# First attention of a two-layer language-model tower: the values of two of eight key tiles in fp16 parts made by GpSimd, with a factor in the row of maxima

## The reference, cut to what matters

```python
scores = jnp.einsum('bshc,bthc->bsth', q, k) * SCALE
A = jax.nn.softmax(scores, axis=2)
u = jnp.einsum('bsth,bthc->bshc', A, val).reshape(B, S, H * C)
return u @ Wout + bout
```

## Time and profile before

| what | value |
|---|---|
| median of three runs | 4917.46 us |
| the profiled execution's own time | 4918.01 us |
| its span | 4916.3 us |
| the first attention, from its first instruction to its last | some 677 to 2853 us |
| PE busy over the span | 4586.0 us, 93% |
| DVE, ACT, POOL busy | 3655.1, 3150.1, 2325.2 us |

### The profile page before, as it was taken

How to read it: one execution, slowest core, us unless ns; L and a number is a source line. 1 busy time by engine, 2 the same in 40 slices (tenths; PEclk the granted TensorE clock), 3 DMA queues, 4 the chain that set the end, 5 groups by cost and what they waited for, 6 DMA issues and landing times. The chain is left out here.

```text
span 4916.3 us, 106442 instructions
## 1 busy us (share of the span) xinstructions
PE 4586.0 (93%) x42579; PEld 2033.3 (41%) x42579; DVE 3655.1 (74%) x6356; ACT 3150.1 (64%) x3450; POOL 2325.2 (47%) x2279
## 2 busy tenths in 40 slices
PE   5999969999999999999999979999999999999965
PEld 3433423333333333333333334444444444444433
DVE  4677756666666666666666678888888888888878
ACT  2444426666666666666666638888888888888844
POOL 3455553333333323233333346666666666666656
PEclk9999979999999999999999979999999999999966
DMA  4212100000000000000000000000000000000001
GB/s 102 69 52 69 35 1 1 1 1 1 1 1 1 1 1 1 1 1 1 1 1 1 1 1 2 2 2 2 2 2 2 2 2 2 2 3 2 2 7 28
DMA packets 43624, 51.44 MB, mean 10 GB/s; under 512 B 33416, under 2 KB 33544, under 8 KB 43144
## 3 DMA queue, kind: packets, MB, share of 16 engines
q1 hardware_dynamic: 40440, 44.03, 3.4%
q10 hardware_dynamic: 2704, 0.72, 0.1%
HBM read 39.73 MB, written 4.19 MB: 9 GB/s over the span
## 5 line engine op out<-in xcount | busy, mean ns | idle before, releaser
L1716 DVE TENSOR_REDUCE a_mp<-psum 128x1 f32<-128x512 f32 x2072 | 1324.8, 685 | 667.8 <-PE psum L1593 654.1
L2442 DVE TENSOR_REDUCE f_mp<-psum 128x1 f32<-128x512 f32 (+2 forms) x2352 | 1472.7, 684 | 187.1 <-PE psum L2264 171.0
L1561 ACT ACTIVATE a_prob<-psum,escale 128x1024 f32<-128x1024 f32 x1024 | 1086.3, 1110 | 524.6 <-PE psum L1642 524.6
L2224 ACT ACTIVATE f_prob<-psum,escale_f 128x1024 f32<-128x1024 f32 x1152 | 1247.2, 1112 | 217.1 <-PE psum L2341 108.4
L1650 PE MATMUL psum<-a_prob,a_v 128*64 128x512 f32 x4104 | 994.2, 605 | 0.0
L2078 POOL TENSOR_SCALAR f_hi<-f_raw,part 128x512 f16<-128x512 f32 x324 | 506.2, 1562 | 393.8 <-ACT f_raw L2182 387.5
L2264 PE MATMUL psum<-f_kf,f_qf 64*128 64x512 f16 (+2 forms) x3658 | 652.6, 307 | 40.1 <-DVE f_mp L2442 31.2
L1481 POOL TENSOR_TENSOR a_u<-a_og,a_inv 128x512 f32<-128x512 f32 x129 | 134.4, 1042 | 1167.4 <-DVE a_inv L1731 1167.4
L2354 PE MATMUL psum<-f_prob,f_vh 128*32 128x512 f32 (+3 forms) x6144 | 614.7, 495 | 9.3 <-DVE f_oc L2464 7.3
L2333 PE MATMUL psum<-f_qf,f_kf 64*128 64x512 f16 (+3 forms) x3074 | 505.5, 327 | 18.9 <-ACT f_og L2187 18.2
L1650 PEld LDWEIGHTS psum<-a_prob,a_v 128*64 128x64 f32 x4104 | 249.0, 136 | 505.1 <-issue 501.5
(11 more groups left out here) (448 smaller groups left out, 6942.4 us busy)
## 6 DMA issues: line engine op xcount, KB each, us to landing
idx<-in_itok_BS_dram SPq DMA_DIRECT2D x36, 512.0 KB, 6.0
idx<-in_itok_BS_dram SPq DMA_DIRECT2D x54, 256.0 KB, 6.9
idx<-in_x_dram SPq DMA_DIRECT2D x18, 256.0 KB, 3.6
a_qh<-a_rowT SPq DMA_DIRECT2D x258, 1.0 KB
out_dram<-h SPq DMA_DIRECT2D x16, 256.0 KB, 2.6
f_qf<-f_rowT SPq DMA_DIRECT2D x130, 4.0 KB, 1.7
wd<-in_L_ffn_Wd_dram SPq DMA_DIRECT2D x2, 256.0 KB
bd<-in_L_ffn_bd_dram ACTq DMA_DIRECT2D x16, 2.0 KB
```

The source lines that it names most:

```text
L1561: act.activation(prob[:, part], k.psum[:, pair:pair + 2].rearrange("p b n -> p (b n)"), ACT.Exp, scale=k.escale[:]).then_inc(s.read, 1)
L1716: dve.tensor_reduce(mp[:, tg % 2, t + 4 * r, c:c + 1], bank_of(j + r), X, ALU.max)\
L2224: act.activation(prob[:, u % NPF], k.psum[:, pair:pair + 2], ACT.Exp, scale=k.escale_f[:])\
L2442: dve.tensor_reduce(side[:, at[0]:at[-1] + 1:step], bank_of(j + r)[:, 0:len(at) * width].rearrange("p (a b) -> p a b", b=width), X, ALU.ma ...
```

## The change

Key tiles 2 and 4 no longer go through fp32. GpSimd makes `ph`, an fp16 copy of their `a_prob`, and `pl`, the fp16 rest (`halve`, 128x1024 each); once per batch it makes the same of `a_v` (`twice`, into `vh`, `vl`). PE forms their values in three pairs of fp16 matmuls (vl by ph, vh by pl, vh by ph). The chunks become `(0, 1), (3,), (2, 5), (4, 6, 7)`, at the same places. A constant `level`, 6 ln 2 divided by the scale of Exp and at most 8192, is added to the row of maxima when it is copied (a `tensor_scalar` in place of the copy), so that the weights come out 64 times larger. On GpSimd `add` now comes one round later than before, directly behind the halving of key tile 2; `prepare_batch` and `split_x` stand behind it, and the halving of key tile 4 behind these. Three semaphores of an earlier phase are used again, and four buffers are cleared at the start.

```diff
-A_PARTS = ((0, 1), (2, 3), (4, 5), (6, 7))
+A_PARTS = ((0, 1), (3,), (2, 5), (4, 6, 7))
+A_PART_OF = {kt: p for p, part in enumerate(A_PARTS) for kt in part}
+A_HALVED = {2: 0, 4: 1}
+A_LEVEL = 6 * math.log(2.0)
+A_LEVEL_MOST = 8192.0
...
+                def twice(b, par, n):
+
+                    here = v[:, par, :, 0]
+                    pool.tensor_copy(vh[:, par], here).then_inc(s.p, 1)
+                    passed(pool, k.seen, s.p, n + 5)
+                    pool.tensor_tensor(vl[:, par], here, vh[:, par], ALU.subtract).then_inc(s.p, 1)
+
+                def halve(G, kt, count):
+
+                    at = A_HALVED[kt]
+                    passed(pool, k.seen, s.read, count)
+                    pool.tensor_copy(ph[:, at], prob[:, kt]).then_inc(s.p_high, 1)
+                    passed(pool, k.seen, s.p_high, n_half(G, kt))
+                    pool.tensor_tensor(pl[:, at], prob[:, kt], ph[:, at], ALU.subtract).then_inc(s.p_low, 1)
...
                 pool.memset(v[:, 1], 0.0).then_inc(s.clear, 1)
-                pool.sem_inc(s.summed, 1)
-                pool.sem_inc(s.scaled, 2)
-                pool.wait_ge(s.clear, 6)
+                pool.memset(ph[:], 0.0).then_inc(s.clear, 1)
+                pool.memset(pl[:], 0.0).then_inc(s.clear, 1)
+                pool.memset(vh[:, 1], 0.0).then_inc(s.clear, 1)
+                pool.memset(vl[:, 1], 0.0).then_inc(s.clear, 1)
...
                 prepare_batch(0, 0, 0)
+                twice(0, 0, 0)
...
                     for x in range(AROUND):
                         G = i * AROUND + x
+                        b = i * 2 + x // HEADS + 1
+                        split_q(G + 2, (x + 2) % 4, n_stream(i, x, "q", 0))
+                        halve(G, 2, n_stream(i, x, "exp", 2))
+                        if G > 1:
+                            add(i * 2 + (x - 2) // HEADS, x % 2, G)
+                        if x % HEADS == 4:
+                            prepare_batch(b, (x // HEADS + 1) % 2, b * 6)
+                        if x % HEADS == 5:
+                            split_x(b, (x // HEADS + 1) % 2, n_stream(i, x, "x", 0))
+                        halve(G, 4, n_stream(i, x, "exp", 4))
                         if x % HEADS == 3:
                             squares(i * 2 + x // HEADS)
-                        if x % HEADS == 4:
-                            b = i * 2 + x // HEADS + 1
-                            prepare_batch(b, (x // HEADS + 1) % 2, b * 4)
-                        for n, kind, of, part in STREAMS[x]:
-                            if kind == "out":
-                                add(i * 2 + (x - 1) // HEADS, (x + 1) % 2, G + 1)
-                            elif kind == "x":
-                                split_x(i * 2 + x // HEADS + 1, (x // HEADS + 1) % 2, n_stream(i, x, kind, part))
-                            elif kind == "q":
-                                split_q(G + of, (x + of) % 4, n_stream(i, x, kind, part))
+                        if x % HEADS == 6:
+                            twice(b, (x // HEADS + 1) % 2, b * 6)
...
                     for kt in A_PARTS[p]:
+                        if kt in A_HALVED:
+                            at = A_HALVED[kt]
+                            pe.wait_ge(s.p_low, n_half(G, kt))
+                            for a, b in ((vl, ph), (vh, pl), (vh, ph)):
+                                for half in range(2):
+                                    last = pe.matmul(ps[A_SUM][halves(half)], lhsT=a[:, bp, kt],
+                                                     rhs=b[:, at, half * HALF:(half + 1) * HALF],
+                                                     start=False, stop=False, skip_group_check=True)
+                            continue
...
-                        dve.tensor_copy(rowT[:, tg % 2], bank_of(j)[0:T].bitcast(FP16)[:, 0:P]).then_inc(s.row_out, 1)
+                        dve.tensor_scalar(rowT[:, tg % 2], bank_of(j)[0:T].bitcast(FP16)[:, 0:P], level[0:T], None, ALU.add)\
+                           .then_inc(s.row_out, 1)
```

More of the change, by code:

```diff
@@ L1 @@
 from contextlib import ExitStack
+import math
 import numpy as np
@@ L704, in layer0 @@
         E = {name: k.sem("l0_" + name) for name in L_EVENTS}
+        k.spent, k.spent_at = [E[name] for name in ("gT", "eg", "wT")], PAIRS_
         def first(pair):
@@ L1345, in attention1 @@
         prob = sb("a1_prob", [P, NPB, S], F32)
+        ph = sb("a1_ph", [P, 2, S], FP16)
+        pl = sb("a1_pl", [P, 2, S], FP16)
+        vh = sb("a1_vh", [P, 2, T, C], FP16)
+        vl = sb("a1_vl", [P, 2, T, C], FP16)
+        level = sb("a1_level", [P, 1], F32)
         un = sb("a1_un", [P, HALF], F32)
@@ L1366, in attention1 @@
         s.q_split = k.sem("a1_q_split")
+        s.p_high, s.p_low, s.level = k.spent
         s.inverse = k.sem("a1_inverse")
@@ L1394, in n_pv, with n_half @@
             return NAV * (G + 1) + p + 1
+        def n_half(G, kt):
+            return k.spent_at + 2 * (G + 1) + A_HALVED[kt] + 1
         def bank_of(j):
@@ L1499, in _ @@
                 pool.memset(v[:, 1], 0.0).then_inc(s.clear, 1)
-                pool.sem_inc(s.summed, 1)
-                pool.sem_inc(s.scaled, 2)
-                pool.wait_ge(s.clear, 6)
+                pool.memset(ph[:], 0.0).then_inc(s.clear, 1)
+                pool.memset(pl[:], 0.0).then_inc(s.clear, 1)
+                pool.memset(vh[:, 1], 0.0).then_inc(s.clear, 1)
+                pool.memset(vl[:, 1], 0.0).then_inc(s.clear, 1)
+                pool.sem_inc(s.summed, 2)
+                pool.sem_inc(s.scaled, 3)
+                pool.sem_inc(s.p_high, 2)
+                pool.sem_inc(s.p_low, 2)
+                pool.wait_ge(s.clear, 10)
                 prepare_batch(0, 0, 0)
+                twice(0, 0, 0)
                 split_x(0, 0, 1)
@@ L1509, in _ @@
                         G = i * AROUND + x
+                        b = i * 2 + x // HEADS + 1
[8 more added lines that the diff above has]
+                        halve(G, 4, n_stream(i, x, "exp", 4))
                         if x % HEADS == 3:
                             squares(i * 2 + x // HEADS)
-                        if x % HEADS == 4:
-                            b = i * 2 + x // HEADS + 1
-                            prepare_batch(b, (x // HEADS + 1) % 2, b * 4)
-                        for n, kind, of, part in STREAMS[x]:
-                            if kind == "out":
-                                add(i * 2 + (x - 1) // HEADS, (x + 1) % 2, G + 1)
-                            elif kind == "x":
-                                split_x(i * 2 + x // HEADS + 1, (x // HEADS + 1) % 2, n_stream(i, x, kind, part))
-                            elif kind == "q":
-                                split_q(G + of, (x + of) % 4, n_stream(i, x, kind, part))
+                        if x % HEADS == 6:
+                            twice(b, (x // HEADS + 1) % 2, b * 6)
+                add(NB - 1, 0, NB * HEADS)
                 add(NB - 1, 1, NB * HEADS + 1)
@@ L1549, in _ @@
                     read_out(0, -1, kind, of + 1, 2 * (n % 2))
-                act.wait_ge(s.clear, 6)
+                act.wait_ge(s.clear, 10)
                 for i in range(NB // 2):
@@ L1559, in _ @@
                                 continue
-                            act.wait_ge(s.pv, n_pv(G - 1, part // 2))
+                            act.wait_ge(s.pv, n_pv(G - 1, A_PART_OF[part]))
                             act.activation(prob[:, part], k.psum[:, pair:pair + 2].rearrange("p b n -> p (b n)"),
@@ L1643, in score, with values @@
                     return last
-                def values(x, p):
+                def values(G, x, p):
                     bp = (x // HEADS) % 2
+                    first, final = A_PARTS[0][0], A_PARTS[-1][-1]
                     for kt in A_PARTS[p]:
+                        if kt in A_HALVED:
[7 more added lines that the diff above has]
+                            continue
                         for half in range(2):
@@ L1651, in values @@
                                              rhs=prob[:, kt, half * HALF:(half + 1) * HALF],
-                                             start=(kt == 0), stop=(kt == T - 1), skip_group_check=True)
+                                             start=(kt == first), stop=(kt == final), skip_group_check=True)
                     last.then_inc(s.pv, 1)
@@ L1659, in _ @@
                 last.then_inc(s.pv, NAV - sum(at >= T for at in A_VALUES_AT))
-                pe.wait_ge(s.clear, 6)
+                pe.wait_ge(s.clear, 10)
                 for n, (kind, of, part) in enumerate(A_START_STREAM):
@@ L1684, in _ @@
                                             pe.wait_ge(s.read, n_stream(i, x, "exp", A_PARTS[p][-1]))
-                                            values(x, p)
+                                            values(G, x, p)
                                         if at == u + T:
                                             pe.wait_ge(s.read, n_stream(i, x - 1, "exp", A_PARTS[p][-1]))
```

(8 more changed lines are left out.)

## The result

The changed kernel takes 4965.4 us (median of four runs, 4964.57 to 4967.77); the kernel before, with one more run of it beside, 4918.08 us. The ratio is 1.0099, with a 95% interval of 1.0087 to 1.0111. So it is slower, by 47 us. The forecast was 4965 us.

A forecast was written before the change was run, and what follows sets the result against it. The prediction took PE, busy 93% of the span, as the bound. It added 57.6 us for rounds x=4 and x=5, took off 15 for the others and added 4.6 for the start: 4918.0 to 4965 us, range 4931 to 5000.

The forecast's parts named there:

- both steps: Time between `a_un` copies from x=4 and x=5, with GpSimd's halving late: 19.45 and 18.27 us, against 17.51 and 16.61 before.
- the price of `split_x`: GpSimd's halving of a key tile, never run before, was priced like this same-shaped pair of instructions: 3.29 us.
- Rival 2: GpSimd's halving is slower beside DVE's reductions and late in ordinary rounds too; 5077 us at 25% more; chance 0.12.
- plain rounds: Rounds without a once-per-batch task: GpSimd's halving ready at 14.98 us, chunk 3 due at 16.18, 1.2 us to spare.
- PE's gain: Key tiles 2 and 4 as fp16 instead of fp32 matmuls: 0.20 us saved per tile, 0.41 per round.
- DVE's wait: Behind the shortened chunk 1, PE waits some 0.25 us per round for a bank of the maxima that DVE must reduce.
- The net: PE's saving less its wait for DVE: 0.16 us kept per round, 15 us over the 96 rounds other than x=4 and x=5.
- The saving at x=2: The round x=2 was counted among the 96 other rounds, each giving back 0.16 us.
- The start: At the start of the attention, four GpSimd memsets come ahead of `prepare_batch`, which everything waits for: 4.6 us.
- PE's wait for `a_pl`: Expected in the profile 32 times, at x=4 and x=5, some 2.1 and 1.8 us each, and none at tile 2.
- Rival 1: GpSimd is in time in every round, only PE's shorter work shows: 4870 us, or 4902 with DVE's wait; chance 0.12.

The follow-up runs named there:

- the smaller load: The changed kernel with one additional GpSimd memset of 1024 columns (0.87 us) per round, between `add` and what follows it: 5006.6 us, ratio 1.0182.
- the larger one: The changed kernel with one additional GpSimd memset of 2048 columns (1.74 us) per round, between `add` and what follows it: 5093.6 us, ratio 1.0358.

## Why the prediction was right

**The view that counted.** The earlier trace rows says that GpSimd was idle for 9.1 us per round, more than was added. The forecast followed GpSimd in order of time instead, and both steps came out within 0.01 us (19.45 and 18.27 forecast, 19.46 and 18.26 measured). The two runs with one task moved show them to be two separate causes, at the places named.

**GpSimd's rates.** The halving had never run; the price of `split_x` held: 1037 and 2130 ns against 1.04 and 2.13 us. Rival 2 (late in plain rounds) fell with it, and the two runs with load show how far away it was: 1.15 us per round. Its time was also summed too high: at 25% more a plain round would be 1.65 - 1.2 = 0.45 us longer than the 16.18 of the forecast, 43 us in 96 rounds and not 59, so 5061 us in place of 5077.

**PE's gain and DVE's wait.** Both exist, and both terms were too small: 0.49 and 0.26 us per round (the runs without halving) where the forecast had 0.41 and 0.25. The first was taken from the distance of weight loads inside a chunk; half of the whole chunk's 1.87 us, from 1719.81 to 1721.68, would have given 0.94 us per fp32 tile in place of 0.85; the fp16 tile takes 0.67 (1255.12 to 1255.79) in place of 0.65. The net, 0.23 in place of 0.16, makes the five plain rounds of each of 16 batches give back 19 us where the sum has 13 (the step behind x=7 included). The saving at x=2 wasn't there: 17.06 in place of the 16.65 that the sum implies is 7 us the other way. That the two cancel, and so that the total came within 1 us, is luck; the mechanism at x=4 and x=5 is not. Of the 7 us, some 3 are the scaling of the mean (below); the rest goes with the short chunk 1, which costs 0.52 us in this round where the forecast had 0.25 (16.85 against 16.33 in the two runs without halvings).

**The start** costs 5.0 us where 4.6 was forecast. The four memsets put `prepare_batch` 4.4 us later (it starts 8.2 us behind the first memset, where it was 3.8). The other 0.6 us come between there and the first `a_un`; that they are the longer first chunk 3 is likely and not shown.

**What the profile would show.** One item was wrong: PE's wait for `a_pl` does not appear 32 times, but at x=5 and, at x=4, in the first batch alone. At x=5 it is 1.5 us and not 1.8, since without the wait the round takes 16.65 us and not 16.45 (the short chunk again); the step of 18.27 goes by GpSimd's chain alone and isn't touched by this. At x=4 the 2.1 us are shared between the transposes' wait for `a_v` and a wait that carries ACT's name. The forecast had seen that `prepare_batch` ends late but had not named its other consumer; with tile 4 last in its chunk that consumer sets the step.

**Rival 1** (only PE's shorter work shows) is what the kernel becomes when the order is mended: 4903.8 us, against the 4902 that the forecast gave it with DVE's wait. That this is so close owes to the same cancelling terms.

## What to carry to other kernels

When a bound engine is made to wait for another, add up the other engine's queue from its last hard wait to the new result, round by round; the mean idle time says nothing about the rounds that also hold a rare task. Ahead of a result that the bound engine waits for, put only what has an earlier due time, and place the wait as late in the consumer's chunk as it goes: the first was worth 62 us here, the second alone 45. A shortened piece of the bound engine's work can uncover a wait for a ring of buffers that another engine empties (here the three banks of the maxima); even pieces were worth 41 us in the kernel without halvings.

## What the runs showed of the hardware

A small VectorE instruction waited for GpSimd. VectorE and GpSimd in order of time, the changed kernel at x=2 in one batch and in another:

```profile
1708.62 0.67 DVE L1792 TENSOR_SCALAR mean_f<-mean_f 128x8 f32<-128x8 f32 x1
```

```profile
1707.14 2.12 POOL L1493 TENSOR_TENSOR a_pl<-a_prob,a_ph 128x1024 f16<-128x1024 f32 x1 [0.18 <-POOL a_ph L1491]
```

```profile
1166.12 0.68 DVE L1790 TENSOR_REDUCE mean_f<-h 128x8 f32<-128x512 f32 x1
1166.84 0.38 DVE L1792 TENSOR_SCALAR mean_f<-mean_f 128x8 f32<-128x8 f32 x1
```

```profile
1165.06 2.13 POOL L1493 TENSOR_TENSOR a_pl<-a_prob,a_ph 128x1024 f16<-128x1024 f32 x1 [0.18 <-POOL a_ph L1491]
```

The same line over all its instructions (ns, min/median/max) in the changed kernel, then in the one without halvings:

```profile
L1792 DVE TENSOR_SCALAR mean_f<-mean_f x17: 172/380/666, 759.9 to 2898.1; 128x8 f32<-128x8 f32 x17
```

```profile
L1789 DVE TENSOR_SCALAR mean_f<-mean_f x17: 171/171/172, 758.5 to 2831.7; 128x8 f32<-128x8 f32 x17
```

With eight elements per partition it takes 0.17 us alone. With GpSimd's subtraction under way it takes 0.38 us in 15 batches and 0.67 in one, as long as the subtraction still has to go: it ends at 1709.29 and 1167.22, GpSimd's instruction at 1709.26 and 1167.19. The reduction ahead of it keeps its 0.68 us, which it also takes without halvings. This agrees with the Trainium skill, SBUF — State Buffer, "Who interferes with whom": a `tensor_scalar` can take the port that VectorE shares with GpSimd, a reduction on trn2 never does. No row shows the port itself. The forecast used only the second half. The delay passes into the step in full: 0.21 us in 15 batches (17.06 against 16.85 in the run without halvings, 17.42 against 17.20 in the first one) and 0.50 us in the one with 0.67 (17.35 against 16.85), together 3.6 us.

TensorE's clock fell to its lower level at x=5 in seven of 16 batches with the smaller load, after waits of 2.06 to 2.42 us, and in all 16 with the larger one, after waits of 2.9 to 3.6 us (there in the first four batches at x=4 too). In the changed kernel it fell in none: its steps at x=5 stay at 18.26 to 18.54 us after waits of up to 1.8 us. A fall at x=5 made its step 1.2 to 1.8 us longer than load alone does. What decides between a fall after 2.42 us and none after 2.42 and 2.71 us stays open.
